# A graph attention and small network kernel: the third layer with its weights stationary in quarters of the PE array

## What is computed

```python
def pipeline(h, W, b):                 # h: nodes x 8 positions x 160 inputs
    for i in range(3):
        h = einsum('bspd,od->bspo', h, W[i]) + b[i]
        if i < 2: h = relu(h)
    return h
y_add, y_sub = pipeline(x_ge, Wa, ba), pipeline(x_ge, Ws, bs)
y = where(m_add, y_add, where(m_sub, y_sub, x_ge))
res_lo, res_hi = round(y[..., 0, 100]), round(y[..., 1, 100])   # clipped to 0..15
carry = round(y[..., 1, 101]) > 0.5
# one-hot rows of res_lo, res_hi and the carry are added to columns 128..160 of the output
```

## Time and profile before

| what | value |
|---|---|
| median of three runs | 3326.24 us (3325.85 to 3329.14) |
| span of the profiled execution | 3328.5 us |
| busy share of the span | PE 88%, DVE 87%, POOL 66%, ACT 66% |
| last stage, from the trace | about 2981 to 3328.5 us |
| a group in the last stage | 13.89 us |

### The profile page before, as it was taken

The page is one execution under the profiler, slowest core; times in us unless marked ns, Lnnn a source line. Parts: engine busy times, 40 slices in busy tenths (PEclk is TensorE's granted clock), DMA queues, the critical chain, the costliest instruction groups (busy, mean ns, idle before and its releaser), DMA issues.

```text
span 3328.5 us, 51387 instructions
## 1 busy us (share of the span) xinstructions
PE 2913.6 (88%) x11922; PEld 1712.5 (51%) x12048; DVE 2900.1 (87%) x8850; ACT 2181.1 (66%) x7642; POOL 2204.1 (66%) x2509
## 2 busy tenths in 40 slices
PE   6897889887988169999999999999999999989999
PEld 4554445554554025555555555555555555555555
DVE  9897777776776279999999999999999999998886
ACT  6432222222221039999999999999999999964443
POOL 0377777777777647777777777777777777741111
PEclk9898888888888589999999999999999999999998
DMA  6344333333332487888888888788888888831221
GB/s 209 80 136 107 106 99 103 103 106 100 103 103 85 166 286 256 255 253 254 257 256 260 253 261 253 254 255 256 255 256 255 260 253 258 256 100 66 76 76 69
DMA packets 259197, 615.22 MB, mean 185 GB/s; under 512 B 69755, under 2 KB 80327, under 8 KB 258642
## 3 DMA queue, kind: packets, MB, share of 16 engines
q0 software_dynamic: 144832, 443.72, 42.3%
q1 hardware_dynamic: 107718, 155.40, 15.5%
q10 hardware_dynamic: 6348, 12.80, 1.1%
HBM read 550.28 MB, written 61.49 MB: 184 GB/s over the span
## 4 chain that ended last, share of the span: by engine, by line
DVE 28%; POOL 25%; issue 20%; PE 15%; DMA 8%; DVEq 2%; another core or an unknown queue 1%; ACT 0%; ACTq 0%; SPq 0%; POOLq 0%
POOL rec_scratch L631 21%; DMA big<-kv_scratch,small 8%; DVE big L1396 7%; DVE small L1289 6%; DVE big L1283 5%; PE banks L1920 5%; POOL big L652 2%; PE banks L1899 2%; PE banks L1982 2%; DVE big L1009 2%; PE banks L1847 1%; POOL small L659 1%; PE banks L1755 1%; DVE big L1014 1%
## 5 line engine op out<-in xcount | busy, mean ns | idle before, releaser
L815 ACT ACTIVATE big<-big,small 128x65 f32<-128x65 f32 x6564 | 1604.3, 338 | 4.8
L652 POOL DMA_INDIRECT big<-kv_scratch,small x832 | 842.3, 1012 | 407.6 <-DVE small L1289 286.5
L631 POOL DMA_INDIRECT rec_scratch<-big,small x782 | 770.6, 985 | 342.2 <-issue 237.7
L1899 PE MATMUL banks<-big,small 128*128 128x260 f32 x3328 | 897.9, 393 | 87.0 <-POOL small L659 45.6
L1847 PE MATMUL banks<-big,small 128*128 x1664 | 873.3, 607 | 34.6 <-DVE big L1283 16.1
L1899 PEld LDWEIGHTS banks<-big,small 128*128 128x128 f32 x3328 | 598.8, 190 | 522.3 <-issue 249.7
L1755 PE MATMUL banks<-big 128*128 128x512 f32 (+1 forms) x1176 | 611.1, 668 | 22.3 <-DVE big L999 22.3
L1396 DVE SCALAR_TENSOR_TENSOR big<-big,loS,banks 128x520 f32 x832 | 611.5, 735 | 5.4 <-PE banks L1899 4.4
L1283 DVE TENSOR_TENSOR big<-banks,big 128x512 f32<-128x512 f32 x832 | 558.8, 672 | 44.7 <-PE banks L1847 24.1
L659 POOL TENSOR_SCALAR small<-iotaF,small 128x128 f32<-128x128 f32 x832 | 525.9, 632 | 50.6 <-PE banks L1899 25.1
L1289 DVE TENSOR_REDUCE small<-big 128x8 f32<-128x512 f32 x832 | 548.8, 664 | 0.0
(11 more groups left out here) (263 smaller groups left out, 2720.4 us busy)
## 6 DMA issues: line engine op xcount, KB each, us to landing
rowR<-lo_rows SPq DMA_DIRECT2D x97, 256.0 KB
big<-src_rows SPq DMA_DIRECT2D x97, 256.0 KB, 3.5
big<-in_x_dram SPq DMA_DIRECT2D x96, 256.0 KB, 2.8
big<-kv_scratch,small POOLq DMA_INDIRECT x832, 5.2
rec_scratch<-big,small POOLq DMA_INDIRECT x782
kv_scratch<-big SPq DMA_DIRECT2D x48, 260.0 KB
q_scratch<-big SPq DMA_DIRECT2D x48, 256.0 KB
kv_scratch<-big SPq DMA_DIRECT2D x48, 256.0 KB
```

Of the source, the lines that this page charges most:

```text
L631: e.indirect_dma_start(recd, bass.IndirectOffsetOnAxis(ap=ridx[:, c % 4, j:j + 1], axis=0), rec[:, 8 * c + j, :], None).then_inc(s_sc[c % ...
L652: e.indirect_dma_start(KV[:, vat(t):vat(t) + YW + D], None, KVd, bass.IndirectOffsetOnAxis(ap=recB[b_ % 4][:, t % 16, 9:10].bitcast(i32), ...
L815: ins = e.activation(heads(Vr(t), h, h + 1), heads(Vr(t), h, h + 1), ACT.Copy, scale=ph[:, h:h + 1])
L1899: ins = e.matmul(YB[t % 2][:, i, :], oh[t % 4], Vr(t)[:, 260 * i:260 * i + 260], start=True, stop=True)
```

## The change

The roles of the two operands are exchanged in the third layer. `M2a` (128 by 32) holds `N2t[:, 0:4]` in its first four columns and zeros. `M2b` (128 by 128) holds block j's four columns at columns 32j to 32j+3 and zeros. Both are filled once, by two memsets and two copies on DVE. In `f_out(g)`, for each block j, `M2a` stands in the quarter 32j of PE's columns, and the 128 columns of block j of `h2[0]` go through; then `M2b` stands in the whole array, and the 128 columns of `h2[1]` go through and are added up. The result, in bank 6, has results on partitions (four used of each 32) and nodes along the row. ACT copies it to `oT` (`f_oc`), and PE turns it into bank 7 by one transpose (`f_ot`), from where `f_posts` reads it with another stride.

`f_out` is no longer in four parts: it stands in one piece behind chunk 0 of the second window's projection and ahead of `f_fq(g + 1)`; `f_ot` stands between chunks 2 and 3. On ACT `f_oc(g)` stands behind the second copy of turned data and ahead of `f_FT(g + 1)`. The third product of the next group's first layer, which writes bank 6 too, now waits for `f_oc`.

```diff
+        M2a = e_(32)
+        M2b = e_(128)
+        oT = [e_(128) for _ in range(2)]
...
             def f_h2r(g, k_):
-                q.wait_ge(s_h3, g)
+                q.wait_ge(s_o3, g)
...
+            def f_oc(g):
+                C = 64 * len(pair(g))
+                q.wait_ge(s_o3, g + 1)
+                q.wait_ge(s_h3, g - 1)
+                e.copy(oT[g % 2][0:C, :], BK[6][0:C, 0:128]).then_inc(s_oc, 1)
...
                 if len(n3) > 1:
                     f_yTe(n3[1])
+                f_oc(g)
                 if n1:
                     f_FT(g + 1)
...
+            e.memset(M2a, 0.0).then_inc(s_w3, 1)
+            e.memset(M2b, 0.0).then_inc(s_w3, 1)
...
-                    e.tensor_tensor(r4, BK[7][0:n, 8 * i:8 * i + 8].rearrange("p (q c) -> p q c", q=2),
+                    e.tensor_tensor(r4, BK[7][0:n, 64 * i:64 * i + 64].rearrange("p (q c) -> p q c", c=32)[:, :, 0:4],
...
             f_stats(pair(0))
             f_feats(pair(0))
+            q.wait_ge(s_fw, 39 * 16)
+            q.wait_ge(s_w3, 2)
+            e.tensor_copy(M2a[:, 0:4], N2t[:, 0:4]).then_inc(s_w3, 1)
+            e.tensor_copy(M2b.rearrange("p (j c) -> p j c", c=32)[:, :, 0:4], N2t[:, 4:20].rearrange("p (j c) -> p j c", c=4)).then_inc(s_w3, 1)
...
             def f_h1(g, k_):
...
                     q.wait_ge(s_h1r, 3 * g)
+                    q.wait_ge(s_oc, g)
...
-                        e.matmul(BK[7][0:n, 4 * j:4 * j + 4], h2[0][:, c0:c0 + n], N2t[:, 0:4], start=True, stop=False)
-                        ins = e.matmul(BK[7][0:n, 4 * j:4 * j + 4], h2[1][:, 0:n], N2t[:, 4 + 4 * j:8 + 4 * j], start=False, stop=True)
...
+            def f_out(g):
+                C = 64 * len(pair(g))
+                q.wait_ge(s_w3, 4)
+                q.wait_ge(s_h2r, 2 * g + 2)
+                q.wait_ge(s_oc, g)
+                for j in range(C // 32):
+                    e.matmul(BK[6][32 * j:32 * j + 32, 0:128], M2a, h2[0][:, 128 * j:128 * j + 128], start=True, stop=False)
+                e.matmul(BK[6][0:C, 0:128], M2b[0:C, 0:C], h2[1][0:C, 0:128], start=False, stop=True).then_inc(s_o3, 1)
+
+            def f_ot(g):
+                C = 64 * len(pair(g))
+                q.wait_ge(s_oc, g + 1)
+                q.wait_ge(s_res, 2 * g)
+                e.transpose(BK[7][:, 0:C], oT[g % 2][0:C, :], ident[0:C, 0:C]).then_inc(s_h3, 1)
...
+                f_out(g)
                 if n1:
                     f_fq(g + 1)
-                f_out(g, (0,))
                 if len(n2) > 1:
-                    f_wo(n2[1], 1, 2)
-                f_out(g, (1,))
-                if len(n2) > 1:
-                    f_wo(n2[1], 2, 3)
-                f_out(g, (2,))
+                    f_wo(n2[1], 1, 3)
+                f_ot(g)
                 if len(n2) > 1:
                     f_wo(n2[1], 3, 4)
-                f_out(g, (3,))
```

More of the change, by code:

```diff
@@ L375, in build @@
         s_fq, s_FT, s_h1, s_h1r, s_h2, s_h2r, s_h3, s_fz, s_res = sem("s_fq"), sem("s_FT"), sem("s_h1"), sem("s_h1r"), sem("s_h2"), sem("s_h2r"), sem("s_h3"), sem("s_fz"), sem("s_res")
+        s_w3, s_o3, s_oc = sem("s_w3"), sem("s_o3"), sem("s_oc")
         def pair(g):
@@ L1987, in f_h2 @@
                 ins.then_inc(s_h2, 1)
[L1989 to L1999, removed]
-                        e.matmul(BK[7][0:n, 4 * j:4 * j + 4], h2[0][:, c0:c0 + n], N2t[:, 0:4], start=True, stop=False)
-                        ins = e.matmul(BK[7][0:n, 4 * j:4 * j + 4], h2[1][:, 0:n], N2t[:, 4 + 4 * j:8 + 4 * j], start=False, stop=True)
-                        if 2 * i + h_ == 2 * len(ws) - 1:
-                            ins.then_inc(s_h3, 1)
+            def f_out(g):
[11 more added lines that the diff above has]
+                e.transpose(BK[7][:, 0:C], oT[g % 2][0:C, :], ident[0:C, 0:C]).then_inc(s_h3, 1)
             q.wait_ge(s_ya, T)
```

## The result

| | median | runs |
|---|---|---|
| before | 3326.05 us | 6 (3318.67 to 3329.14) |
| changed | 3310.7 us | 6 (3303.43 to 3314.56) |

The ratio is 0.9951, with a 95% interval of 0.9938 to 0.9965: the changed kernel is faster by 0.5%, by 16 us with an interval of 12 to 21. The forecast was 3304.8 us, a gain of 21.4, with a range of 3298 to 3314. The time is in the range and the sign is right; the gain is smaller than forecast by a quarter.

What follows compares the result with a forecast made beforehand. PE was taken to bound groups 0 to 21. Gains of 1.015 us in each of 21 groups (21.3) and 0.57 in group 21 make 21.9, less 0.45 at the start 21.4, from 3326.24 to 3304.8 us; range 3298 to 3314.

Steps and rivals of the forecast that it cites:

- What bounds: Last stage, groups 0 to 21: PE sets the pace, busy 13.82 of 13.89 us; DVE waits for it once a group.
- The old third layer, 1.77 us: PE's time in a full group for the four parts of the old third layer: 1.77 us.
- The new third layer, 0.755 us: PE per group: switch to quarters 0.105, quarter products 0.26, full product with going back 0.28, transpose 0.11; sum 0.755 us.
- the eight quarter records took longer than 0.3 us: Sign that the prediction is wrong, in the new third layer on PE; it had reckoned 0.26 us for these records.
- Group 21, 0.57 us: Only three old parts, about 1.33 us, stood on group 21's path; less 0.755, it gains 0.57 us.
- The drain: Changes between whole array and quarters on PE cost 0.165 us for a pair, already in the sum.
- The cover: Time to spare before moved steps delay PE: 0.94 us at `f_out` and `f_fq`, 1.5 at `f_ot`, 1.8 behind ACT's copy.
- The start, 0.45 us: Start of the stage: DVE's two memsets and two copies stand ahead of line 1464, so PE loses 0.45 us.
- The end, 0: Groups 22 to 24, where PE is short of work: taken as 0, give or take 1 us.
- The quarters do not run one after another: Rival for the new third layer's quarter products: run in turn, 22 groups lose 10.5 us, 3337 us; chance 0.03.
- The clock didn't fall in group 22: Rival at the program's end: the clock falls already in group 22, doubling up to 9.56 us of PE work, 3314; chance 0.05.
- first rival: The full product of `M2b` waits for the quarters' results, two waits of 0.4 us a group: gain 13 us, 3313; chance 0.11.

Runs made afterwards that it cites:

- run 7: Kernel before with three of the four parts of its old third layer left out: a group is 12.55 us, 1.34 less than 13.89.
- run 10: Kernel before with its old third layer in one piece at the new place, behind chunk 0 and ahead of `f_fq`: a group is 13.89 us.
- run 9: Changed kernel with group g - 1's third layer behind group g's second-layer quarters: ratio to before 0.9991; groups 12.19 and 12.79 us, later 13.3 to 14.8.
- run 5: Changed kernel with the four quarter products issued four times over, 32 records instead of 8: a group is 13.73 us.
- run 12: Run 9's kernel with ten instead of eight buffers for x and loads one pair earlier: median 3305.49 us, ratio to before 0.9942.
- run 6: Changed kernel with three idle ACT copies ahead of the new copy in each group: a group stays at 13.08 us.
- runs 4: Changed kernel with `M2a` held four times, so each quarter loads from its own columns: a group is 13.08 us.
- run 8: Kernel before again, unaltered: groups of 13.89 us, 304.77 us for the 22, and an end of 26.50 us.
- run 3: Changed kernel with `M2b`'s product written to other columns of bank 6 and not added to the quarters' result: groups of 13.08 us.
- run 2: Changed kernel with the full product of `M2b` split into four 32 by 32 products: a group is 13.11 us, ratio 0.9971.

## Why the prediction was right in sign, and where it was off

- **What bounds.** Right. PE sets the group before and after, and still does at 12.55 us (run 7). DVE's wait shrank by what the group did.
- **The old third layer, 1.77 us.** Right: run 7 gives 1.79, run 10 1.77 in one piece, and the group without a third layer (run 9) 1.70, to which the 0.06 us of the chunk behind the features' transposes comes, named in the next point.
- **The new third layer, 0.755 us.** This is the term that failed: it is 1.77 less 0.82, some 0.95. Two of its lines were too small and one was missing; going over to quarters (0.105) and the transpose (0.11) were right. The quarters were taken at 0.033 us a record from a burst of 24; but a burst has 0.13 us on top of its rounds, which the 24 shared and the eight bear alone, so they take 0.35 and not 0.26 (run 5). The full product was taken from records of a transpose and takes 0.33 and not 0.28. And the chunk that now stands right behind the features' transposes takes 0.06 more (1.78 for 1.71), a term that the sum didn't have. Together 0.20 us, by 22 groups 4.4: of a forecast of 21.4 these leave 17. The prediction had said that it would be wrong if the eight quarter records took longer than 0.3 us, and this sign came.
- **Group 21, 0.57 us.** Up to the second layer of group 22 it gained 0.82 as the others did (13.08 to 12.26), which brings the 17 back towards 17.7. Some of it can be lost again behind that point; the end varies too much to show it.
- **The drain.** The sum had 0.165 us for a pair of switches. The 0.13 us that a burst pays once come on top of it. Run 9's second group and run 12 show both: with one burst in a group instead of two, and otherwise the same products, a group is 0.29 us shorter (13.08 to 12.79), as 0.165 and 0.13 make. The Trainium skill says that changing the tiling mode drains PE, without a price (TensorEngine Tiling (Array Packing), Key Properties); these 0.29 us agree with it.
- **The cover.** Right in each place: no wait at `f_out`, `f_fq` or `f_ot`, and 1.4 us more on ACT change nothing in groups 0 to 21 (run 6).
- **The start, 0.45 us.** It was 0.33 (13.54 to 13.87). In three of the ten traces with a new third layer (runs 4, 6 and 12) the stretch was 15.6 to 15.7 us: there the granted clock was 0.62 to 0.64 in the 4 us of group 0's first products. None of the four traces with the old one has that, and neither has any of the three of the unaltered changed kernel; whether the new start has a part in it is not shown.
- **The end, 0.** It varies by 3 us with the clock in both kernels; at the same number of stretches at half the clock it differs by 0.1 to 0.4 us (run 8), so 0 was right.
- **Rivals.** The full product does not wait for the quarters' results (run 3). The quarters do not run one after another, so the rule that a load overlaps running products only where the row groups differ (the Trainium skill, TensorE: Matmul & The Clock Gate, Part 3) doesn't fit these quarters, all of which use all rows: 32 records took 1.01 us, and one after another they would have taken 7 by the prediction's 0.219 a record. The clock didn't fall in group 22: in the first trace it stayed full up to 3290. The exchange does do what it says (run 10).

By the traces, 17.99 less 0.33 gives 17.7 us for the change, and a few tenths more at the end where the clock is alike. The measured gain of 16 us (11.6 to 20.6) agrees with that, and the forecast's 21.4 lies just outside. The time alone couldn't have told the forecast from its first rival (a wait for the quarters, 13 us): it lies between the two. That the rival is out, and which terms were short, the group and run 3 show. So the path and the sign were right by the mechanism; that the time fell inside the range is owed in part to the room that the range left for that rival.

## What to carry to other kernels

A record with four columns going through took 0.11 us here, no less than one of the transposes with 128 (0.11): what it costs is the 128 by 128 block that stands. Exchange the operands, and the long side goes through while the short side stands. When a cost per record is read from a long burst, look for what the burst pays once, above all if the new burst is a third as long. And two quarter bursts pay for their switches twice (0.29 us a group here): bring them together, but then follow the result to its store, to the load that waits for it, and to the end of the program, where late steps have nothing to hide behind.

## What the runs showed of the hardware

- A burst of quarter products (128 columns through, 32-bit) has rounds of four records at 0.11 us and 0.13 us once: 0.35, 0.79 and 1.01 us for 8, 24 and 32 records.
- Eight records of 32 by 32 blocks take the same 0.35 us as eight of 128 by 32, and behind such a burst start as late as a full product does, 0.36 us after its first record (run 2).
- What the full product writes to, and adds to, doesn't change that start (run 3: 0.36 us as well).
- The kernel before takes 3535 us on one chip and 3324 to 3327 in all other sets of runs; the difference lies ahead of the last stage; a group of the changed kernel's last stage is the same 13.07 to 13.08 us on all of them.
